# Constant products on TensorE in front of its waits, in a transformer layer with routed experts

## The chip, the cores and the metric

The kernel runs on one core of one Trainium2 chip. The metric is the time of one execution on the device, in microseconds (us), as the median of several runs. The engines are TensorE (PE; its weight loads are PEld), VectorE (DVE), ScalarE (ACT), GpSimd (POOL) and SyncE (SP), which issues most of the DMAs. TensorE's clock has two levels here, 1.2 and 2.4 GHz; the profile gives the granted level as a share of the full one (0.50 or 1.00).

## The reference

It is one transformer layer on 8 sequences of 256 tokens of width 256. Cut to what matters:

```
mod = (silu(c) @ wmod)                   # six rows a sequence: shifts, scales, gates
h = layernorm(x) * (1 + ca) + sa
q, k, v = h @ Wq.T, h @ Wk.T, h @ Wv.T   # 8 heads, 2 of keys and values, 32 wide
q, k = rope(q), rope(k); q, k, v = each normalised over its 32
p = softmax(30 * tanh((q k / sqrt(32) + mask) / 30))   # causal, window of 64
x = x + ga * ((p v) @ Wo)
h = layernorm(x) * (1 + cb) + sb
choose 4 of 16 experts for each token (best 2 of 4 groups first)
x = x + gb * (sum over the chosen of weight * expert(h) + shared expert(h))
```

## The kernel before

**Two stages.** The first function, `attention`, runs attention, the second layer norm and the choice of experts. After it all engines meet, and `experts` runs the experts. 2048 tokens are 16 tiles of 128.

**Attention** is a software pipeline over the sequences b, written out by hand: `step(b)` for b from -2 to 8. On each engine's queue one step mixes work of four sequences: `ahead` (b+2: transpose and modulate the normalised input, project it to q, k, v), `lead` (b+1: rotate, normalise, transpose q and k), `here` (b: scores, tanh, exp, times v) and `lag` (b-1: transpose the attention output, multiply by Wo, residual, layer norm, transpose, router logits). An engine's queue is strictly in order, and semaphores join the queues, so the order below is what sets the time.

PE's step is, in order: `turn_xhat(b+2)` (L807); scores of the first head group (L852 mask, L855, L858); four transposes of the attention output (L906); scores of the second group; twelve products with Wo (L791 to L793 through `split3`, which writes a float32 product as three); `weigh` of the first group (probabilities times v, L878 to L883); `project(b+2)` (L791 to L793); `weigh` of the second group; `turn_qk(b+1)`, which waits for the normalised keys (`k_done`) and transposes k (L828) and q (L838); then for `lag` a wait for the second layer norm's output (`h2_done`) and for ACT's copy of q (`qt_done`), four transposes (L941), a wait for ACT's copy of them (`h2t_done`), a wait for DVE's last attention output (`attn_done`), in steps 3, 5, 6, 7 and 8 a count of chosen rows (`count_before`, L1051 and L1052), and the router logits (L952).

DVE's step runs rotation and centring (L619 to L630), the low part of the attention output (`otl`, L726, which needs ACT's `oth`, which needs PE's L906), the residual (L669, which needs PE's Wo product), layer norms, the normalised q and k, and, in the steps named in `CHOSEN`, the 25 or so small instructions of `choose`; a step later `place_rows` (L1059 on), which needs PE's count through ACT's copy. POOL computes the powers for the norms (L431 and others), half of the rotation (L427), splits weights in the first steps, and sends rows to their experts' places in device memory (L1073).

Before PE can multiply a tile by routed weights, the last two tiles of rows must be counted (`count_before` at u = -2 of `experts`), DVE works out tables of tiles, and PE spreads them over the partitions (L1481, at u = 0). The units u are pairs of a tile and an expert: 16 units of shared tiles first, then 80 routed tiles, then 16 units of shared tiles.

**The tiles that the change touches.** `sc_ps` holds the scores: four PSUM banks of 512 float32 columns, of which columns 0 to 319 (`SC` = 320) are used. `up` holds two banks for an expert's first product, of which columns 0 to 351 are used. `ident` is the 128 x 128 identity, `mask_f` the float32 mask. Both are float32, and a plain float32 product is made of two instructions in the trace (x2 for one product).

Of the kernel before, what the change touches and what calls it, by code (L numbers as in the profile page):

```python
# [18 lines left out]
P = 128  # L19
B, S, HID = 8, 256, 256  # L20
# [4 lines left out]
REP = H // KV  # L25
# [10 lines left out]
E, INTER, TOPK, G, TOPK_G = 16, 176, 4, 4, 2  # L36
# [44 lines left out]
K1, K0, SC = 128, 192, 320  # L81
# [43 lines left out]
GROUPS = [(0, 4), (4, 4), (8, 2), (10, 2), (12, 2), (14, 2)]  # L125
LAST = len(GROUPS) - 1

CHOSEN = {3: 0, 5: 1, 6: 2, 7: 3, 8: 4}
SENT = {4: (0, 1), 5: (2, 3), 6: (4, 5), 7: (6, 7, 8), 8: (9, 10, 11)}

# [8 lines left out]
for _m in range(len(GROUPS) + 1):  # L139
    for _step in (ROUTE1 + " " + ROUTE2 if _m <= LAST else TABLES).split():  # L140
        _name, _, _times = _step.partition("*")
# [112 lines left out]
def attention(nc, a, mod_rows, x1d, rows_d, hrow, gate_t, ident, w, r):  # L254
    with ExitStack() as ctx:
# [521 lines left out]
        def _(pe):  # L777
# [6 lines left out]

            counted = pv[:, QT * E:3 * QT * E].rearrange("p (t e) -> p t e", e=E)

            def split3(out_ap, xh, xl, wh, wl):

                n = len(xh)
                for k in range(n):  # L790
                    pe.matmul(out_ap, xh[k], wh[k], start=(k == 0), stop=False)  # L791
                    pe.matmul(out_ap, xh[k], wl[k], start=False, stop=False)
                    mm = pe.matmul(out_ap, xl[k], wh[k], start=False, stop=(k == n - 1))  # L793
                return mm
# [13 lines left out]
                mm.then_inc(s.xhat_t, 1)  # L808

            def project(b):  # L810
                pe.wait_ge(s.htl_done, b + 1)
                pe.wait_ge(s.hth_done, (b + 1) * KC)
                if b == 0:
                    pe.wait_ge(s.wqkvl_done, 1)
                after(pe, s.qkv_done, b)
                after(pe, s.kt_done, b - 1)
                after(pe, s.gated_done, b - 2)
                for t in range(QT):
                    mm = split3(qkv_ps[:, t, 0:QKV], [hth[:, c, t * P:(t + 1) * P] for c in range(KC)], [htl[:, c, t * P:(t + 1) * P] for c in range(KC)],
                                [wqkvh[:, c] for c in range(KC)], [wqkvl[:, c] for c in range(KC)])  # L820
                mm.then_inc(s.qkv_mm, 1)

            def turn_qk(b):
                pe.wait_ge(s.k_done, (b + 1) * QT * KV)
                pe.wait_ge(s.qkv_done, min(b + 2, B))
                for t in range(QT):
                    for c in range(KV):
                        mm = pe.transpose(qkv_ps[:, 0, c * S + t * P:c * S + (t + 1) * P], kn[:, t, c].rearrange("p r d -> p (r d)"), ident[:])  # L828
                mm.then_inc(s.k_t, 1)
                pe.wait_ge(s.q_done, b + 1)  # L830
                if b + 1 < B:
                    pe.wait_ge(s.ht_done, (b + 2) * KC)
                    pe.wait_ge(s.hth_done, (b + 2) * KC)
                after(pe, s.oth_done, b - 1)
                after(pe, s.otl_done, b - 1)
                for t in range(QT):
                    for c in range(KV):
                        mm = pe.transpose(tp[:, c, t * P:(t + 1) * P], qn[:, t, c * P:(c + 1) * P], ident[:])  # L838
                mm.then_inc(s.q_t, 1)
# [46 lines left out]
            def step(b, ahead, lead, here, lag):  # L886
                if ahead:
                    turn_xhat(b + 2)
                if b == B:
                    pe.wait_ge(s.gate_done, b - 1)  # L890
                    pe.wait_ge(s.attn_done, 2 * b)
                    pe.wait_ge(r.placed, LAST - 1)
                    count_before(pe, r, g, counted, LAST - 1).then_inc(r.counted, 1)
                if here:
                    scores(b, b % 2, 0)
# [35 lines left out]
                if lead:  # L931
                    turn_qk(b + 1)
                if lag:
                    pe.wait_ge(s.h2_done, b)
                    if lead:
                        pe.wait_ge(s.qt_done, b + 2)
# [5 lines left out]
                    mm.then_inc(s.h2_t, 1)  # L942
                    pe.wait_ge(s.h2t_done, b)
                    if here:
                        pe.wait_ge(s.attn_done, 2 * b + 2)
                    else:
                        pe.wait_ge(r.placed, LAST)
# [128 lines left out]
def experts(nc, a, out, mod_rows, x1d, rows_d, y_d, hrow, gate_t, tab, w, r, ident):  # L1076


    with ExitStack() as ctx:
# [316 lines left out]
        def _(pe):  # L1396
            held = {}

            def load_expert(u):
                kind, i = jobs[units[u][0]]  # L1400
                if kind == "routed":
                    held[u] = nc.values_load(tab.expert[0:1, i:i + 1], engines=[mybir.EngineType.PE], min_val=0, max_val=E - 1,
                                             skip_runtime_bounds_check_because="held to E - 1 when worked out")
# [65 lines left out]
            def step(u):  # L1469
                if starts(u + 2):  # L1470
                    turn_x(units[u + 2][0])
                if 0 <= u < N:
                    up_mm(u)
                if u == -2:
                    count_before(pe, r, g, counted, LAST)
                    pe.wait_ge(r.worked, WORKED["cum", QT, LAST])
                    pe.matmul(totals, r.ones[:], r.cum[:, NT], start=True, stop=True).then_inc(r.counted, 1)
                if u == 0:
                    pe.wait_ge(r.worked, WORKED["cols", 2, LAST + 1])
                    for j in range(2):  # L1480
                        mm = pe.matmul(spread_ps[:, j], cols[0:TILES, j:j + 1].to_broadcast([TILES, P]), ident[0:TILES, 0:TILES], start=True, stop=True)  # L1481
                    mm.then_inc(s.spread, 1)
# [50 lines left out]
```

## Time and profile before

| | |
|---|---|
| median of 3 runs | 552.26 us (552.13 to 553.73) |
| the profiled execution | 552.77 us, its span 550.9 us |
| mean granted clock | 0.83 |
| PE, PEld busy | 416.4 us (76%), 379.5 us (69%) |
| DVE busy | 388.4 us (71%) |
| POOL, ACT busy | 286.8 us (52%), 234.2 us (43%) |

The span is from the first to the last instruction of the profiled execution. Its time lies 1.9 us above its span. The attention stage ends at about 274 us, the steady part of the experts runs from about 306 to 500 us, and the rest collects and stores. A busy engine in the profile isn't always one that sets the time: the question at every point is which wait ends last.

### The profile page before, as it was taken

The numbers are of one execution on the slowest core, as the hardware profiler recorded it, in microseconds if no ns is written. First come the engines' busy times: TensorE is split into PE (matmuls) and PEld (weight loads), VectorE is DVE, ScalarE is ACT, GpSimd is POOL, SyncE is SP. The second block draws the span as 40 slices with busy tenths as digits, with TensorE's granted clock in tenths as the row PEclk, the third lists the DMA queues.
The fourth block names the chain that finished last, engine by engine and source line by source line (L and its number), as shares of the span: only waits on it lengthen the run. The fifth ranks groups of instructions, "written<-read, shape, count | busy, mean of one in ns | idle before, by whom it ended". The sixth has DMA issues, their size and how long they took to land.

```text
span 550.9 us, 10571 instructions
## 1 busy us (share of the span) xinstructions
PE 416.4 (76%) x2841; PEld 379.5 (69%) x2841; DVE 388.4 (71%) x1158; ACT 234.2 (43%) x554; POOL 286.8 (52%) x278
## 2 busy tenths in 40 slices
PE   2447896966598586774234999999999999996752
PEld 2335875846486465563234998999999999986752
DVE  1663798778897968185482788777777777754998
ACT  1334362443257150400122676666666666653220
POOL 1545655633588748363376332444444444444992
PEclk9975686879598766565657899999999999999797
DMA  8404012030215122721283333444444444446962
GB/s 308 131 2 149 0 47 94 1 95 1 93 45 180 43 92 78 271 94 54 70 304 130 91 114 94 142 137 144 138 141 142 143 143 139 152 121 230 397 236 73
DMA packets 38294, 69.68 MB, mean 126 GB/s; under 512 B 5720, under 2 KB 27864, under 8 KB 38112
## 3 DMA queue, kind: packets, MB, share of 16 engines
q1 hardware_dynamic: 31328, 49.08, 28.0%
q0 software_dynamic: 6912, 19.93, 9.7%
q8 instruction: 27, 0.44, 0.3%
q14 instruction: 27, 0.22, 0.1%
HBM read 42.49 MB, written 26.51 MB: 125 GB/s over the span
## 4 chain that ended last, share of the span: by engine, by line
issue 18%; POOL 13%; DVE 8%; PE 6%; DMA 3%; another core or an unknown queue 2%; ACT 0%; POOLq 0%; DVEq 0%; SPq 0%; ACTq 0%
POOL y_d L1211 13%; DMA y_d<-yout,to 2%; DVE yt L1319 2%; DMA yt<-y_d 1%; PE up L1439 1%; DVE f_htl L1303 1%; PE up L1440 1%; PE up L1441 1%; DVE hid L1299 1%; PE xt_ps L1422 1%; DVE yt L1316 1%; DVE yt L1312 1%; PE y_ps L1463 0%; DVE f_xl L1274 0%
## 5 line engine op out<-in xcount | busy, mean ns | idle before, releaser
L1211 POOL DMA_INDIRECT y_d<-yout,to x80 | 76.7, 959 | 90.8 <-ACT yout L1246 90.0
L1073 POOL DMA_INDIRECT rows_d<-hrow,slots x64 | 65.6, 1026 | 35.5 <-issue 16.5
L1296 DVE SCALAR_TENSOR_TENSOR hid<-silu,xin,up 128x64 f32<-128x64 f32 (+1 forms) x160 | 47.2, 336 | 23.0 <-PE ht_ps L1449 16.3
L1225 ACT ACTIVATE f_xh<-xt_ps 128x256 fp32r<-128x256 f32 x96 | 36.9, 384 | 57.0 <-PE xt_ps L1422 43.6
L1230 ACT ACTIVATE silu<-up 128x176 f32<-128x176 f32 x112 | 35.6, 318 | 58.5 <-PE up L1441 44.9
L1439 PE MATMUL up<-w_routed,f_xh 128*128 x160 | 58.3, 364 | 0.0
L431 POOL TENSOR_TENSOR rn<-meansq,minus_half 128x24 f32<-128x24 f32 x8 | 33.4, 4175 | 39.5 <-DVE meansq L637 39.4
L1441 PE MATMUL up<-w_routed,f_xh 128*128 x160 | 51.7, 323 | 0.0
L1440 PE MATMUL up<-w_routed,f_xl 128*128 x160 | 51.6, 323 | 0.0
L1274 DVE TENSOR_TENSOR f_xl<-xt_ps,f_xh 128x256 fp32r<-128x256 f32 x96 | 40.6, 423 | 10.4 <-ACT f_xh L1225 4.2
L1303 DVE TENSOR_TENSOR f_htl<-ht_ps,f_hth 128x256 fp32r<-128x256 f32 x112 | 46.6, 417 | 0.0
L1235 ACT ACTIVATE f_hth<-ht_ps 128x256 fp32r<-128x256 f32 x112 | 43.1, 385 | 4.0 <-PE ht_ps L1449 3.7
L1463 PE MATMUL y_ps<-w_shared,f_hth 112*128 112x256 f32 x32 | 12.5, 391 | 26.6 <-DVE f_htl L1303 26.5
L1246 ACT ACTIVATE yout<-y_ps 128x256 f32<-128x256 f32 x80 | 30.5, 381 | 4.0 <-DMA y_d<-yout,to 3.0
L1449 PE MATMUL ht_ps<-ident,hid 128*128 128x128 f32 x112 | 30.8, 275 | 0.0
L1448 PE MATMUL ht_ps<-ident,hid 128*128 128x128 f32 x112 | 30.7, 274 | 0.0
L1422 PE MATMUL xt_ps<-ident,xin 128*128 128x128 f32 x160 | 30.5, 272 | 0.0
L1440 PEld LDWEIGHTS up<-w_routed,f_xl 128*128 128x128 f32 x160 | 30.4, 190 | 0.0
L1439 PEld LDWEIGHTS up<-w_routed,f_xh 128*128 128x128 f32 x160 | 30.2, 189 | 0.0
L1463 PE MATMUL y_ps<-w_routed,f_hth 112*128 x80 | 29.2, 365 | 1.2 <-DVE f_htl L1303 1.0
L1441 PEld LDWEIGHTS up<-w_routed,f_xh 128*128 128x128 f32 x160 | 30.0, 188 | 0.0
L233 POOL TENSOR_TENSOR w_routed<-raw,w_routed 128x960 fp32r<-128x960 f32 x9 | 20.2, 2243 | 16.7 <-ACT w_routed L1252 16.3
(259 smaller groups left out, 1335.3 us busy)
## 6 DMA issues: line engine op xcount, KB each, us to landing
xin<-rows_d SPq DMA_DIRECT2D x80, 144.0 KB
yt<-y_d SPq DMA_DIRECT2D x16, 512.0 KB, 10.3
raw<-in_w_raw SPq DMA_DIRECT2D x13, 608.0 KB
mod<-mod_rows SPq DMA_DIRECT2D x8, 384.0 KB, 3.5
w_stage<-in_w_raw SPq DMA_DIRECT2D x5, 608.0 KB, 4.1
rows_d<-zeros SPq DMA_DIRECT2D x16, 144.0 KB
x<-in_x SPq DMA_DIRECT2D x4, 512.0 KB, 8.2
x1d<-x SPq DMA_DIRECT2D x8, 256.0 KB
```

What stands on the lines that cost most here:

```text
L1073: pool.indirect_dma_start(rows_d, bass.IndirectOffsetOnAxis(ap=r.slots[:, t, k:k + 1], axis=0), hrow[:, t], None).then_inc(r.sent[t // QT] ...
L1211: pool.indirect_dma_start(y_d, bass.IndirectOffsetOnAxis(ap=to[:, i:i + 1], axis=0), yout[:, i % YR], None)\
L1225: act.activation(xh[:, j % XB], xt_ps[:], ACT.Copy).then_inc(s.xh, 1)
L1235: act.activation(hth[:, u % 2].rearrange("p c q -> p (c q)"), ht_ps[:, u % 2, 0:2 * P], ACT.Copy).then_inc(s.hth, 1)
L1274: dve.tensor_tensor(xl[:, j % XB], xt_ps[:], xh[:, j % XB].bitcast(F32), ALU.subtract).then_inc(s.xl, 1)
L1296: dve.scalar_tensor_tensor(out=hid[:, u % HB3, to_cols], in0=silu[:, u % 2, cols], scalar=weight, in1=y, op0=ALU.mult, op1=ALU.mult).then_ ...
L1303: dve.tensor_tensor(htl[:, u % 2].rearrange("p c q -> p (c q)"), ht_ps[:, u % 2, 0:2 * P], hth[:, u % 2].rearrange("p c q -> p (c q)").bit ...
L1422: mm = pe.transpose(xt_ps[:, c], src[:, c * P:(c + 1) * P], ident[:])
L1439: pe.matmul(o, xh[:, j % XB, c], wh, start=(c == 0), stop=False)
L1440: pe.matmul(o, xl[:, j % XB, c], wh, start=False, stop=False)
L1441: mm = pe.matmul(o, xh[:, j % XB, c], wl, start=False, stop=(c == KC - 1))
L1463: pe.matmul(o, hth[0:HA, q, 0], at(HA, O2A, O2B), start=begin, stop=False)
```

## The change

A helper `fill(n)` issues n matrix products whose operands are constants and whose output columns nothing reads. In attention one is the identity times 192 columns of the float32 mask, into columns 320 to 511 of the last bank of `sc_ps`; in `experts` it is the identity times itself, 128 columns, into columns 352 to 479 of the second bank of `up`. They carry no semaphore and no wait of their own. They stand on PE's queue in front of waits that PE already had:

- before `project(1)`: 8
- in `turn_qk`, before the wait for the keys: 6 in step -1, 12 in steps 3 and 5, 6 in step 6
- before the wait for `h2_done`: 6 in steps 1 to 7, 12 in step 8
- after the wait for `h2t_done`, before the wait for `attn_done`: 3 in steps 1 to 7
- in step 8, before the count of group 4 and after its other waits: 12
- in `experts`: 16 before the count of the last group (u = -2), 8 before the wait for the tables' columns (u = 0)

```diff
+WAITS_K = {-1: 6, 3: 12, 5: 12, 6: 6}
...
+            def fill(n):
+                for _ in range(n):
+                    pe.matmul(sc_ps[:, REP - 1, SC:512], ident[:], mask_f[:, 0:512 - SC], start=True, stop=True, skip_group_check=True)
...
             def project(b):
+                if b == 1:
+                    fill(8)
                 pe.wait_ge(s.htl_done, b + 1)
...
             def turn_qk(b):
+                fill(WAITS_K.get(b - 1, 0))
                 pe.wait_ge(s.k_done, (b + 1) * QT * KV)
...
                     pe.wait_ge(r.placed, LAST - 1)
+                    fill(12)
                     count_before(pe, r, g, counted, LAST - 1).then_inc(r.counted, 1)
...
                 if lag:
+                    fill(6 if b < B else 12)
                     pe.wait_ge(s.h2_done, b)
...
                     pe.wait_ge(s.h2t_done, b)
                     if here:
+                        fill(3)
                         pe.wait_ge(s.attn_done, 2 * b + 2)
...
+            def fill(n):
+                for _ in range(n):
+                    pe.matmul(up[:, 1, 2 * INTER:2 * INTER + P], ident[:], ident[:], start=True, stop=True, skip_group_check=True)
...
                 if u == -2:
+                    fill(16)
                     count_before(pe, r, g, counted, LAST)
...
                 if u == 0:
+                    fill(8)
                     pe.wait_ge(r.worked, WORKED["cols", 2, LAST + 1])
```

## Rows read from the trace of the kernel before

**Rows 1.** The page, the granted clock in 40 equal slices, in tenths
```profile
PEclk9975686879598766565657899999999999999797
```

**Rows 2.** Busy time by stretch: PE, PEld, DVE, ACT, POOL, granted clock, DMA
```profile
87.40:101.00 13.60, 11.00 (x65) 7.80 (x66) 9.11 (x15) 7.25 (x11) 2.27 (x5) 0.50 0.28 95
101.10:114.60 13.50, 10.40 (x85) 9.93 (x83) 11.91 (x28) 3.59 (x6) 12.78 (x11) 1.00 0.01 2
...
210.40:234.10 23.70, 16.86 (x94) 13.18 (x94) 9.75 (x41) 7.32 (x10) 11.91 (x12) 0.50 0.58 203
```

**Rows 3.** Whom PE waited for, 60 to 300: total, times, longest
```profile
PE tp L941 <- DVE hrow L698: 17.2, 5, 5.9
PE qkv_ps L828 <- DVE kn L651: 15.9, 3, 6.8
```

**Rows 4.** PE in order of time, steps 1 and 2: start, us, what [idle before]
```profile
88.28 1.12 PE L941 MATMUL tp<-ident,hrow 128*128 128x128 f32 x4 [2.76 <-DVE hrow L698]
90.80 1.86 PE L952 MATMUL pv<-wgate,late 128*128 128x16 f32 x8 [1.40 <-DVE attn L663]
92.50 1.09 PE L807 MATMUL tp<-ident,xhat 128*128 128x128 f32 x4
93.38 1.27 PE L852 MATMUL sc_ps<-mask,ident_b 128*128 128x320 bf16 x4
...
97.40 1.25 PE L852 MATMUL sc_ps<-mask,ident_b 128*128 128x320 bf16 x4 [0.31 <-ACT capped L519]
...
99.95 0.58 PE L791 MATMUL qkv_ps<-woh,oth 128*128 128x256 f32 x1
```

**Rows 5.** PE in order of time, step 4 and the start of 5
```profile
153.84 0.72 PE L852 MATMUL sc_ps<-mask,ident_b 128*128 128x320 bf16 x4 [0.78 <-issue]
...
155.25 0.39 PE L791 MATMUL qkv_ps<-woh,oth 128*128 128x256 f32 x1
...
166.54 0.63 PE L941 MATMUL tp<-ident,hrow 128*128 128x128 f32 x4 [0.89 <-ACT qt L507]
167.86 1.07 PE L952 MATMUL pv<-wgate,late 128*128 128x16 f32 x8 [0.69 <-ACT late L565]
168.77 0.63 PE L807 MATMUL tp<-ident,xhat 128*128 128x128 f32 x4
169.24 1.18 PE L852 MATMUL sc_ps<-mask,ident_b 128*128 128x320 bf16 x4
```

**Rows 6.** ACT in order of time, step 2
```profile
96.11 1.24 ACT L519 ACTIVATE capped<-sc_ps 128x1280 f32<-128x1280 f32 x1 [0.55 <-PE sc_ps L858]
```

**Rows 7.** DVE in order of time: the waits that PE's work ends
```profile
97.86 0.69 DVE L726 TENSOR_TENSOR otl<-tp,oth 128x512 fp32r<-128x512 f32 x1 [3.58 <-ACT oth L546]
...
102.16 0.69 DVE L669 TENSOR_TENSOR late<-qkv_ps,mod 128x512 f32<-128x512 f32 x1 [1.24 <-PE qkv_ps L793]
...
123.10 0.69 DVE L726 TENSOR_TENSOR otl<-tp,oth 128x512 fp32r<-128x512 f32 x1 [3.57 <-ACT oth L546]
...
197.76 0.22 DVE L1059 TENSOR_TENSOR place<-placed,small 128x64 f32<-128x64 f32 x1 [4.25 <-ACT placed L513]
...
234.45 0.69 DVE L669 TENSOR_TENSOR late<-qkv_ps,mod 128x512 f32<-128x512 f32 x1 [4.28 <-PE qkv_ps L793]
...
261.19 0.69 DVE L669 TENSOR_TENSOR late<-qkv_ps,mod 128x512 f32<-128x512 f32 x1 [3.02 <-PE qkv_ps L793]
```

**Rows 8.** PE in order of time, step 1: float32 products of 132 columns
```profile
76.63 0.39 PE L878 MATMUL pv<-v,masked 128*128 128x132 f32 x2
76.86 0.97 PE L880 MATMUL pv<-v,probs 128*128 128x33 f32 x8
```

**Rows 9.** PE in order of time, ahead of the routed tiles
```profile
280.16 0.19 PE L1051 MATMUL route_ps<-cum,ones 128*128 128x32 bf16 x1 [5.49 <-DVE cum L1028]
...
287.28 1.14 PE L1481 MATMUL route_ps<-ident,l_cols 80*128 80x80 f32 x4 [2.70 <-DVE l_own_e L1350]
```

**Rows 10.** ACT in order of time, the second stage's start
```profile
300.24 0.32 ACT L1230 ACTIVATE silu<-up 128x176 f32<-128x176 f32 x1 [8.02 <-remote]
```

## The prediction, made before the changed kernel was run

> **What bounds the kernel now.** I read the granted clock over the span first. It is full in the experts' steady part, but in attention and up to about 306 us it falls again and again to half [rows 1]. The table by stretch shows what surrounds a fall: at half clock from 87.4 to 101.0 PE was busy 11.00 of 13.6 us, at full clock from 101.1 to 114.6 10.40 of 13.5 [rows 2]. So a slow stretch is not one in which PE had little to do: it is one that follows a gap. The list of waits names the gaps: 17.2 us in 5 waits for DVE's `hrow` ahead of L941, 15.9 us in 3 waits for `kn` ahead of L828 [rows 3]. PE sits idle there, the clock falls, and the products behind the gap run at 1.2 GHz. The logits that end step 1 start at 90.80 and step 2's L807 at 92.50, 1.70 us later; at the end of step 4, at 2.4 GHz, the same takes 167.86 to 168.77, 0.91 us [rows 4, 5].
>
> Slow PE work costs only where another engine waits for it. DVE's own order of time shows where: in step 2 it waits 3.58 us ahead of `otl`, which hangs on PE's L906 through ACT, and 1.24 us ahead of the residual, which hangs on the Wo product; in step 3, 3.57 us; in step 6, 4.25 us for the placed rows; in step 7, 4.28 us and in step 8, 3.02 us for the Wo product [rows 7]. Between these waits DVE is the bound, and PE's clock is of no account. A mean clock of 0.83 over 550.9 us is 94 us of clock lost, but it can't come back as 94 us of time: I count the waits alone.
>
> **What a fill costs.** The nearest row is L878, a float32 product of 132 columns, which takes 76.63 to 76.86, 0.23 us, at 2.4 GHz [rows 8]. In proportion to columns, 192 are 0.33 us and 128 are 0.22 us; at 1.2 GHz twice that, 0.67 and 0.45. So at full clock 3 fills are 1.0, 6 are 2.0, 8 are 2.7, 12 are 4.0 us; the experts' 16 are 3.6 and 8 are 1.8 us. Bounds: if weight loads rather than columns paced them, all would cost the 0.23 of the row, down to 1.4 us for 6; and double at half clock.
>
> What lies over them: L941 of step 1 waits 2.76 us and the logits 1.40 more [rows 4], so 2.0 and 1.0 are hidden. L941 of step 4 waited only 0.89 us [rows 5]: there 6 fills stand out by 1.1 us and 3 more by 1.0, since the three come behind ACT's copy and the logits had waited for nothing else. The 12 in front of the keys lie in waits of up to 6.8 us [rows 3]. The 16 of the experts lie in 5.49 us and the 8 in 2.70 us [rows 9]; at half clock they would be 7.1 and 3.6, that is 1.6 and 0.9 too long. The 8 ahead of `project(1)` and the 6 of step -1 stand before POOL's and DVE's long start-up, off the path either way: 0.
>
> **What a full clock gives**, if the fills hold it:
> - Step 2, up to `otl`: the logits and L807 take 2.58 us at half clock (90.80 to 93.38) and 1.38 at full (167.86 to 169.24) [rows 4, 5]: 1.2. ACT's tanh then no longer waits 0.55 for the scores [rows 6]. Together 1.75. The wait of 1.24 ahead of the residual goes too, since the second scores fall from 2.55 (97.40 to 99.95) to 1.41 (153.84 to 155.25). Sum 3.0.
> - Step 3: the same first part, 1.75.
> - The waits for placed rows at the start of steps 4, 6, 7 and 8 (4.25 in step 6 [rows 7]): the logits and L941 ahead of them give back 0.8 and 0.45 each, the 3 fills take 1.0, and where 6 fills stand out by 1.1 the faster transposes of q and k return about that. I count 1.5 for the four; the bounds are 5.0 (no fill in the way) and -3 (each stands out in full while the clock is slow).
> - Step 7: first scores 1.15, second scores 1.15, the Wo product 1.2 of the 4.28 [rows 7]: 3.5.
> - Step 8: of the 3.02 behind `otl` the twelve products are nearly all, 1.2 of it comes back; L906 0.3. Sum 1.5. The last L941 and logits count nothing: the wait ahead of them is 5.9 us [rows 3], 12 fills fill 4.0, and the clock may well have fallen again.
> - Start of the experts: L1481 0.57 of its 1.14 [rows 9], and as an estimate 0.9 from the first dozen products behind it, whose kind halves as L852 does. Sum 1.5.
>
> All of it is 12.75 us. Steps 2 and 3 I take whole, 4.75, because PE's clock was full ahead of their gaps [rows 2, 8] and need only be held. The rest, 8.0, I take at half: there the clock has to be won back first, gaps of 2 to 3 us stay even with the fills, and each slow fill costs double. That is 4.0, in all 8.75. From the profiled execution's 552.77 this gives 544.0; the median of the runs lies 0.5 lower, so 543.5 us. The experts' steady part isn't touched, since it runs at full clock with PE full, and everything behind shifts by what the start gains.
>
> The Trainium skill, TensorE: Matmul & The Clock Gate, Part 1 (The HAM clock gate), has a rule that speaks against this: it puts the ramp penalty below 1% of a typical kernel's span. By that rule this change could give no more than 5.5 us, 546.8 or above; rows 1 show falls all through attention, not one ramp, so the trace agrees with it only for the experts' steady part.
>
> **Rivals.**
> - *A small gain or none.* The fills don't hold the clock: PE does only short transposes ahead of and behind them, and a 6.8 us wait with 4.0 us of fills still has 2.8 idle. For it: the clock fell behind 114.6 although PE had been busy for 10.40 of the 13.5 us before [rows 2]. Against: fills are as dense as work gets. Steps 2 and 3 then give half, 2.4, and of the rest what the standing out of fills takes: 549.5, and 547.5 to 552 around it. This is also the case in which the change doesn't do what it says. The skill's rule above is of this kind; its own bound is 546.8.
> - *A stall goes as well.* ACT's silu at 300.24 comes after 8.02 idle us that the trace can't put down to an engine [rows 10], though the unit's products take only some 2 us. If it hangs on the order of events, a new timing may lose it: 8 us more and about 1.5 that PE's clock loses in it, 534. Against: nothing in the change aims at it.
> - *Slower.* The fills are issued while the clock is at 1.2 GHz and stay so: 6 take 4.0 us against 0.89 of wait in step 4 [rows 5] and, as I take it, in 5 and 6 (3.1 each, 9.4), and 3 take 2.0 in about five steps (10): 552.3 + 19 = 571. It decides where a fill run lasts longer than its wait, above 2.8 us for steps 1 and 2. Against: in each gap of steps 1 and 2 the clock is still full when the fills begin.
>
> **How the numbers follow.** Forecast (539 to 547.5) 0.55; stall gone too 0.17; small gain or none 0.20, half of it within 0.3% (1.7 us, about what a measurement can tell from no change); slower 0.08. So faster 0.82, same 0.10, slower 0.08. The range runs from 532 (all of the 12.75 and most of the stall) to 551.
>
> **What would show it.** In the changed kernel's profile the clock row should read 9 or more over most of attention; L952 to L807 should be about 0.9 us apart in every step; DVE's waits of rows 7 should shrink to about 1.8, 0, 1.8, 4, 1 and 1.8 us; L941 should start later behind L838 in steps 4 to 6, by about 1 us. The prediction is wrong if the clock still falls in steps 4 to 8, if the gain in DVE's waits is eaten by new waits for POOL's powers (L431) or for `placed`, or if the 8 us stall moves.

## The result, and the profile after

The changed kernel took 561.16 us (560.11 to 564.62, 4 runs) against 552.96 us for the kernel before (552.13 to 553.73, 4 runs). The ratio is 1.0157, interval 1.0129 to 1.0185: 8.2 us slower, where 9 us less was forecast. The profiled execution has a span of 559.2 us, against 550.9. Here and below the ratios leave out executions more than 1.5% above the fastest of their kernel and the medians do not, so a ratio need not be the quotient of the medians beside it.

The granted clock did what it was meant to do up to about 190 us, and in part behind that. The page of the changed kernel, its clock row and the group of the fills (262 float32 instruction records, 377 ns mean):

```profile
PEclk9989689999999886667877799999999999999787
...
L792 PE MATMUL sc_ps<-mask_f,ident 128*128 128x192 f32 x262 | 57.0, 377 | 6.3 <-ACT late L567 5.8
```

Where [rows 1] have 5 to 9, slices 6 to 15 (of 14.0 us each) read 9 and 8 now, while 16 to 23 still read 6 to 8. The stretches (columns as in [rows 2]) say the same in numbers: at full clock from 87.4 to 187 us, 0.72 behind that.

```profile
87.40:101.00 13.60, 10.88 (x102) 8.79 (x100) 11.11 (x18) 8.63 (x12) 4.26 (x6) 1.00 0.26 94
...
140.00:187.00 47.00, 38.97 (x331) 35.21 (x332) 38.23 (x115) 20.30 (x29) 35.06 (x35) 1.00 0.31 105
187.00:234.00 47.00, 36.94 (x220) 33.13 (x220) 22.24 (x75) 10.28 (x16) 21.72 (x20) 0.72 0.38 129
```

DVE's own waits, which answer to [rows 7], show both halves of the story: the two waits ahead of `otl` fell from 3.58 and 3.57 to 1.58 us, and the waits for the placed rows (`place`, which stands behind L941, now L953, and the logits) grew, one of them to 14.27 us. Line numbers of the changed kernel are higher by up to some 20.

```profile
96.65 0.69 DVE L728 TENSOR_TENSOR otl<-tp,oth 128x512 fp32r<-128x512 f32 x1 [1.58 <-ACT oth L548]
118.44 0.69 DVE L728 TENSOR_TENSOR otl<-tp,oth 128x512 fp32r<-128x512 f32 x1 [1.58 <-ACT oth L548]
195.31 0.23 DVE L1072 TENSOR_TENSOR place<-placed,small 128x64 f32<-128x64 f32 x1 [5.79 <-ACT placed L515]
...
232.12 0.19 DVE L1072 TENSOR_TENSOR place<-placed,small 128x32 f32<-128x32 f32 x1 [14.27 <-ACT placed L515]
...
257.69 0.19 DVE L1072 TENSOR_TENSOR place<-placed,small 128x32 f32<-128x32 f32 x1 [6.74 <-ACT placed L515]
```

What holds the second of these `place` is seen in PE's and ACT's order of time. First PE of the changed kernel (L792 are the fills, L838 and L848 the transposes of the keys and queries):

```profile
213.33 4.19 PE L792 MATMUL sc_ps<-mask_f,ident 128*128 128x192 f32 x12
217.31 1.06 PE L838 MATMUL qkv_ps<-ident,kn 128*128 128x128 f32 x4
218.16 0.71 PE L848 MATMUL tp<-ident,qn 128*128 128x128 f32 x4
218.71 2.12 PE L792 MATMUL sc_ps<-mask_f,ident 128*128 128x192 f32 x12
225.94 1.08 PE L953 MATMUL tp<-ident,hrow 128*128 128x128 f32 x4 [5.12 <-ACT qt L509]
227.71 2.29 PE L792 MATMUL sc_ps<-mask_f,ident 128*128 128x192 f32 x6 [0.69 <-ACT late L567]
```

then ACT, whose copies of the transposed keys and queries L953 waits for:

```profile
223.81 0.60 ACT L507 ACTIVATE kt<-qkv_ps 128x512 f32<-128x512 f32 x1 [20.21 <-remote]
225.20 0.60 ACT L509 ACTIVATE qt<-tp 128x512 f32<-128x512 f32 x1 [0.79 <-remote]
```

The keys' transposes end at 218.37 and ACT had been idle for 20 us, but it starts its copy at 223.81. Its releaser reads `remote`: the trace finds no engine's increment there in time. The semaphore events of the trace tell more. The increment that L838's last instruction makes is recorded at 223.73, 5.4 us after that instruction's end, and L848's at 225.18, 6.3 us after 218.87. The increments of ACT, DVE and POOL that can be matched stand 0.01 us behind the ends of their instructions (median; none is over 0.04), and so do nearly all of PE's. I call such increments of PE late. The ends of PE's products in the profile are modelled, so the trace doesn't tell a product that truly finished late from an increment that was passed on late; but PE itself had gone on to the next instructions (L848 at 218.16, the fills at 218.71).

The same thing in the experts' first units: the products of the second unit end at 295.80, their increment comes 11.6 us later, and ACT's silu answers to the stall of [rows 10] with twice its length.

```profile
291.15 0.32 ACT L1243 ACTIVATE silu<-up 128x176 f32<-128x176 f32 x1
307.43 0.32 ACT L1243 ACTIVATE silu<-up 128x176 f32<-128x176 f32 x1 [15.96 <-remote]
```

The kernel before has them too: products that end between 292.4 and 293.8 have increments 6.6 to 7.8 us late, all at 300.2 to 300.4. That is the stall of [rows 10]; in attention it has three, 1.1 to 2.1 us late, of products that end between 223 and 227.

### The profile page after: what moved, and what is told of

It is laid out like the page before. It is cut to its first block and busy times, and to the rows that moved or that the text cites. A ratio compares the mean times of both kernels' runs of the same rounds, so it can differ in the third digit from the quotient of the medians.

```text
span 559.2 us, 11187 instructions
## 1 busy us (share of the span) xinstructions
PE 448.9 (80%) x3151; PEld 418.6 (75%) x3151; DVE 388.4 (69%) x1158; ACT 233.6 (42%) x554; POOL 285.8 (51%) x278
## 5 line engine op out<-in xcount | busy, mean ns | idle before, releaser
L1224 POOL DMA_INDIRECT y_d<-yout,to x80 | 76.7, 959 | 90.9 <-ACT yout L1259 89.8
L1309 DVE SCALAR_TENSOR_TENSOR hid<-silu,xin,up 128x64 f32<-128x64 f32 (+1 forms) x160 | 47.2, 336 | 23.2 <-PE ht_ps L1467 19.7
L792 PE MATMUL sc_ps<-mask_f,ident 128*128 128x192 f32 x262 | 57.0, 377 | 6.3 <-ACT late L567 5.8
L792 PEld LDWEIGHTS sc_ps<-mask_f,ident 128*128 128x128 f32 x262 | 51.7, 225 | 8.2 <-ACT late L567 7.7
L1457 PE MATMUL up<-w_shared,f_xh 128*128 128x352 f32 x64 | 23.6, 369 | 12.4 <-DVE hid L1312 12.4
L1457 PEld LDWEIGHTS up<-w_routed,f_xh 128*128 128x128 f32 x160 | 30.2, 189 | 0.0
```

Of the source, the lines that this page charges most:

```text
L792: pe.matmul(sc_ps[:, REP - 1, SC:512], ident[:], mask_f[:, 0:512 - SC], start=True, stop=True, skip_group_check=True)
L1224: pool.indirect_dma_start(y_d, bass.IndirectOffsetOnAxis(ap=to[:, i:i + 1], axis=0), yout[:, i % YR], None)\
L1309: dve.scalar_tensor_tensor(out=hid[:, u % HB3, to_cols], in0=silu[:, u % 2, cols], scalar=weight, in1=y, op0=ALU.mult, op1=ALU.mult).then_ ...
L1457: pe.matmul(o, xh[:, j % XB, c], wh, start=(c == 0), stop=False)
```

## The experiments

Runs that were made together met the same chip, and each ratio is against the kernel before on that chip. The chips turned out not to be alike, so each run names its chip (A, B, C, D); which one the first result was made on isn't on record. A table comes first: the lengths in the trace from one L941 to the next (1 to 2 is from step 1's to step 2's, and so on), from step 8's L941 to the choice that starts the experts, from there to the first send of y, and the rest. The start-up ahead of step 1's L941 varies from 87.2 to 91.0 us from one execution to another (step6 has 90.5, step6_2, the same kernel, 87.4) and is left out. It isn't without effect on what follows: without early fills 1 to 2 takes 25.4 or 25.5 where it was 87.4 to 88.6, and 23.6 to 24.0 in the three profiles where it was 90.1 to 90.9 (before_zeros, step6_late, step6).

```
              chip  1-2   2-3   3-4   4-5   5-6   6-7   7-8  choice  y send  rest
before         -    25.4  31.2  21.6  27.1  25.8  26.7  20.9   7.0    63.4   213.5
after          -    21.8  29.5  21.8  29.3  34.5  26.0  22.0   7.0    65.9   212.4
exp_only       A    25.5  31.3  21.6  27.1  25.8  26.7  20.9   7.0    64.5   217.8
att_only       A    21.7  29.5  24.2  29.1  31.6  27.1  21.3   7.0    63.1   213.8
early5         A    21.8  29.5  24.2  27.7  26.5  25.0  20.9   7.0    63.6   212.0
wide           A    21.8  32.1  23.8  27.3  32.8  24.9  19.7   7.0    63.4   213.2
bf16           A    21.8  29.5  21.7  30.3  35.1  28.0  22.6   7.0    66.4   212.5
after_zeros    A    21.8  29.5  21.8  29.0  35.1  28.0  22.0   7.0    65.7   213.2
after_sends    A    21.8  29.5  21.8  30.4  35.2  26.0  26.8   7.0    65.3   212.3
before_zeros   A    23.6  31.5  21.7  27.9  26.7  25.8  20.9   7.0    63.2   213.2
before_2       D    25.4  31.2  21.6  27.1  25.8  26.8  20.9   7.0    63.4   212.8
early5_2       D    21.8  29.5  21.8  29.3  26.7  24.5  21.0   7.0    63.9   211.5
before_late    B    25.4  31.2  21.6  27.1  25.6  24.0  20.8   4.2    91.5   214.7
step6_late     B    24.0  33.2  21.6  27.1  26.5  20.8  20.8   4.2    90.7   212.0
step6          B    23.8  31.5  21.7  26.8  26.3  21.0  20.9   7.0    57.0   213.5
few_wide       B    21.8  31.6  21.7  28.9  25.4  22.4  20.9   7.0    60.0   211.9
step6_2        C    25.5  31.3  21.6  27.1  26.5  21.0  20.9   7.0    59.7   211.4
few_wide_2     C    21.8  29.5  23.2  28.6  25.4  22.4  21.0   7.0    60.0   211.5
after_2        C    21.8  29.5  21.8  29.3  29.1  21.1  19.0   7.0    60.5   211.8
wide_2         C    23.9  31.7  23.8  29.0  28.5  20.9  22.7   7.0    58.7   212.4
```

**One half each.** att_only keeps the fills in attention, exp_only those of the experts:

```diff
 # att_only
-                    fill(16)          # u == -2
-                    fill(8)           # u == 0
 # exp_only: all fill(...) of attention taken out
```

> The fills of attention alone; those in front of the two waits of the experts stage are gone. In the changed kernel the steps up to 5 gain (the logits of step 4 start 3.4 us sooner), step 6 then loses: the increments of TensorE that follow the transposes of k and q at 217 to 219 us arrive 5.4 and 6.3 us after the recorded ends. Theory late signals (TensorE's increments come late while GpSimd sends rows back to back, and the more instructions TensorE has issued in that time the later): step 6 loses as before and the stall at the start of the experts goes back to about 8 us, so about 559 us. Theory overhang (the fills simply outlast their waits, the late increments are a coincidence of one trace): the loss of step 6 is about 2 us, so 555 to 557 us.

> The 16 and 8 fills of the experts stage alone. Theory late signals: the stall begins one or two units sooner, since 24 float32 products are 96 more instructions while GpSimd sends 16 times in a row; its end is tied to GpSimd's last send. Loss 2 to 4 us, 555 to 557 us. Theory overhang: 16 fills outlast their wait by at most 1.6 us and part of that is hidden, the products behind run at 2.4 GHz: 552 to 553.5 us.

Measured: att_only 559.44 against 553.57, 1.0093 (1.0062 to 1.0124); exp_only 554.20 against 553.57, 1.0013 (0.9989 to 1.0036). The loss is mostly attention's, from 5 to 6 on. The experts' fills are worth nothing by the ratio and cost time in the traces: 1.1 us up to the first send of y when they stand alone (64.5 against 63.4), 2.8 on top of attention's (65.9 against 63.1). They run when the clock has mostly fallen, at 0.58 from 281.3 to 287.6. The changed kernel, ahead of the routed tiles:

```profile
281.30 6.28 PE L1415 MATMUL up<-ident 128*128 128x128 f32 x32
287.42 0.18 PE L1064 MATMUL route_ps<-cum,ones 128*128 128x32 bf16 x1
...
290.22 1.95 PE L1415 MATMUL up<-ident 128*128 128x128 f32 x16
```

**Only the early steps.** early5 leaves out what stands behind step 5, and the experts' fills.

```diff
-                fill(WAITS_K.get(b - 1, 0))
+                fill(WAITS_K.get(b - 1, 0) if b - 1 <= 5 else 0)
-                    fill(12)
-                    fill(6 if b < B else 12)
+                    fill(6 if b <= 5 else 0)
-                        fill(3)
+                        fill(3 if b <= 5 else 0)
```

> Fills of attention in steps -1 to 5 alone, none from step 6 on and none in the experts stage. Both theories: the gain of about 3 us that the changed kernel has at the end of step 4 is kept in part (its step 5 loses 1.8 us of it by six fills that stand out behind the transposes of q). Theory late signals: 550 to 551.5 us. Theory overhang: the same. If it is at 552.5 or above, a gain in front of step 6 is always absorbed later.

Measured: 552.43 against 553.57, 0.9948 (0.9905 to 0.9991). The ten executions spread from 546.01 to 558.34, and these medians are only 0.2% apart, so the whole gain isn't firm. In the lengths the gain is plain and stands in the first steps (21.8 and 29.5 against 25.4 and 31.2); with what is put in from step 6 on, the changed kernel loses more than that. One thing is seen at L952's fills of step 3, the same three in both kernels. early5:

```profile
142.34 2.29 PE L792 MATMUL sc_ps<-mask_f,ident 128*128 128x192 f32 x6 [0.69 <-ACT late L567]
144.42 0.26 PE L1063 MATMUL pv<-cum,ones 128*128 128x64 bf16 x1
```

and the changed kernel:

```profile
141.70 1.24 PE L792 MATMUL sc_ps<-mask_f,ident 128*128 128x192 f32 x6 [0.69 <-ACT late L567]
142.78 0.19 PE L1064 MATMUL pv<-cum,ones 128*128 128x64 bf16 x1
```

Three fills cost 2.08 us at half clock and 1.08 at full; where the clock happens to stand when they begin is worth 2.4 us in 3 to 4 (24.2 against 21.8).

**Fewer and more instructions for the same columns.** If the late increments depend on how many instructions PE issues, fewer and wider fills should lose less, and more of them more. wide makes them of 512 columns (3/8 of the instructions in attention, 1/4 in the experts); bf16 makes four bf16 products of each, which is twice the instructions that a float32 product leaves in the trace, over the same columns.

```diff
 # wide
-                for _ in range(n):
-                    pe.matmul(sc_ps[:, REP - 1, SC:512], ident[:], mask_f[:, 0:512 - SC], ...)
+                for _ in range((3 * n + 4) // 8):
+                    pe.matmul(sc_ps[:, REP - 1, :].rearrange("p (a n) -> p a n", n=P), ident[:], ident[:].unsqueeze(1).to_broadcast([P, 4, P]), ...)
 ... # experts: n // 4 of 512 columns
 # bf16
+                if n:
+                    pe.wait_ge(s.mask_set, 2)
+                for _ in range(4 * n):
+                    pe.matmul(sc_ps[:, REP - 1, SC:512], ident_b[:], mask[:, 0:512 - SC], ...)
 ... # experts: 4 * n of r.before[:], r.before[:]
```

> The same places and about the same TensorE time, but each fill is one product of 512 columns (the identity four times) where there were 8/3 of 192, or 4 of 128: 3/8 or 1/4 of the instructions. Theory late signals with instructions as the load: the lateness of step 6 shrinks from 6.3 to 1 or 2 us and the stall of the experts back to about 8 us: 553 to 555 us. Theory overhang: TensorE's time is the same, so 561 us.

> The changed kernel with each float32 fill replaced by four bf16 products of the same columns (constants of bf16): the same columns through the array, twice the instructions. If the number of TensorE's instructions while GpSimd sends is what delays its increments, step 6 loses 10 us or more and the stall begins sooner: 565 us or more. If only columns or time count, 561 us, as the changed kernel.

Measured: wide 555.88 against 553.57, 1.0071 (1.0038 to 1.0104); bf16 569.45 against 552.89, 1.0319 (1.0277 to 1.0360). In the order of instructions it reads wide, changed kernel, bf16: 1.007, 1.016 (1.020 on chip A with the zero writes moved, below), 1.032. Step 6's late increments of the keys and queries are 1.3 and 3.8, 5.4 and 6.3, 7.5 and 7.1 us. Two things weaken the upper end. The profiled executions of bf16 and of the changed kernel with the zero writes moved are alike (spans 564.3 and 564.0 us, 35.1 us from 5 to 6 in both), and bf16 was not run on a chip without late increments, so its other costs aren't separated. The experts' part of wide is no proof either, since its stall (7.89 us ahead of one silu) is as long as that of the kernel before.

**Is it SyncE's zero writes?** They run at that time too. Two runs move the 16 writes of `rows_d` on SyncE's queue ahead of its loads of sequence 2 and later: after_zeros in the changed kernel, before_zeros in the kernel before.

```diff
+            sp.wait_ge(s.zeros_set, 1)
+            for e in range(E):
+                sp.dma_start(rows_d[e * CAP:e * CAP + P], zeros[:]).then_inc(s.heads_zeroed, 16)
             for b in range(2, B):
...
-            sp.wait_ge(s.zeros_set, 1)
-            for e in range(E):
-                sp.dma_start(rows_d[e * CAP:e * CAP + P], zeros[:]).then_inc(s.heads_zeroed, 16)
```

> The changed kernel with SyncE's 16 writes of zeros moved from the end of its attention queue (218 to 228 us, beside GpSimd's 12 sends in a row) to before its loads of step 2. If the backlog of small transfers delays TensorE's increments and the zeros are the larger part of it, the 5.4 and 6.3 us of step 6 fall below 1 us and the time to 553 to 555 us. If GpSimd's sends alone do it, the increments stay 5 to 6 us late and the time at 560 to 562 us. The stall at the start of the experts stage, where no zeros are written, stays in both.

> The same move of the zeros in the kernel before. If the zeros delay the increments, its own late ones at 223.2, 225.6 and 226.6 us (1.5, 2.1 and 1.1 us) go: 549 to 551 us. If the sends alone do it, no change, 552 to 554 us.

Measured: after_zeros 564.29 against 552.89, 1.0202 (1.0146 to 1.0258); before_zeros 553.97, 1.0018 (0.9984 to 1.0052). The late increments stay: 3.6 to 4.5 us in step 6 of after_zeros, where silu's stall is 16.00 us, and up to 3.1 at 227 to 230 in before_zeros. The zero writes aren't needed for them.

**Is it POOL's sends?** All late increments (over 0.1 us) lie in times when POOL sends rows one behind the other: in each of the 12 profiles that have them three or more sends start in the 8 us ahead of such an increment, the last of them at most 4.0 us ahead. In step 6 of the changed kernel there are 12 sends with 0.30 us between them, from 208 to 223 us, the first and the last of them:

```profile
208.02 1.06 POOL L1086 DMA_INDIRECT rows_d<-hrow,slots  x1 [0.18 <-DVE sig L998]
...
222.21 0.96 POOL L1086 DMA_INDIRECT rows_d<-hrow,slots  x1 [0.30 <-issue]
```

and the keys' late increment comes at 223.73. after_sends moves the sends of tiles 4 and 5 from step 6 to step 7. step6_late and before_late move all sends of tiles 4 to 11 behind attention; step6 is the partner of step6_late and has the fills of step 6 alone.

```diff
 # after_sends
-SENT = {4: (0, 1), 5: (2, 3), 6: (4, 5), 7: (6, 7, 8), 8: (9, 10, 11)}
+SENT = {4: (0, 1), 5: (2, 3), 7: (4, 5, 6, 7), 8: (8, 9, 10, 11)}
 # step6_late, before_late
+SENT = {4: (0, 1), 5: (2, 3)}
-for t in range(12, NT):
+for t in range(4, NT):
 # step6: WAITS_K = {6: 6}, fill(6) and fill(3) in step 6 only, no other
```

> The changed kernel with GpSimd's eight sends of tiles 4 and 5 moved from step 6 to step 7, so that nothing is sent while TensorE runs the fills of step 6 and transposes q and k. If the sends (with or without the zeros) delay the increments, the 5.4 and 6.3 us at 218 us go, and part of it comes back in step 7, where 16 sends now stand in a row: 554 to 560 us. If the sends have nothing to do with it, 561 us with the same late increments.

> The kernel before with the fills of step 6 alone: 6 before the keys, 6 before h2_done, 3 before attn_done. Theory late signals: the whole loss of step 6 is here, the increments behind the transposes of k and q are 3 to 6 us late, the time from L941 of step 5 to L941 of step 6 grows from 25.8 to about 32 us: 558 to 561 us. Theory that the late increments need the clock or the shift that the earlier fills bring: 555 us or less.

> The same fills of step 6, but GpSimd sends tiles 4 to 11 in the experts stage with the last four, so that it sends nothing from step 6 on in attention (the experts stage then waits longer for its rows; the total says nothing alone). Theory late signals by sends: in step 6 and later no increment is over 0.3 us late, and step 6 takes at most 2 us longer than in the kernel before with sends moved in the same way. If the fills alone delay the increments, they are 3 to 6 us late as before.

> The control: the kernel before with the sends of tiles 4 to 11 moved to the experts stage. Theory late signals: its own late increments of 1.1 to 2.1 us at 223 to 227 us go and the attention stage ends about 3 us sooner, at about 271 us; at the start of the experts the stall becomes much longer, since 48 sends in a row take 60 us: 30 us or more over the kernel before in total. Otherwise the attention stage ends at 274 us as before.

Measured: after_sends 566.73 against 552.89, 1.0242 (1.0198 to 1.0286). It tells nothing of its question, since POOL still sent one behind the other from 210 to 225 us, and the keys' and queries' increments are 5.5 and 5.1 us late; it only made 7 to 8 longer (26.8). The other three met chip B and gave a surprise. The kernel before took 545.70 us there, not 553, step6 542.72, 0.9961 (0.9937 to 0.9985), step6_late 573.97 and before_late 575.68 (1.0560 and 1.0594, the price of sends that no longer hide behind attention). And in none of the three is a single matched increment of PE late by over 0.06 us, step6 with all its sends in place included. So these don't answer the question of the sends either; they raise that of the chip. In before_late, the kernel before with no late increments, the second stage starts like this:

```profile
284.88 0.32 ACT L1230 ACTIVATE silu<-up 128x176 f32<-128x176 f32 x1 [5.37 <-PE up L1441]
...
286.54 0.32 ACT L1230 ACTIVATE silu<-up 128x176 f32<-128x176 f32 x1
```

The releaser is PE's product by name, not `remote`, and the 8 us stall of [rows 10] isn't there.

**The same kernels on other chips.** few_wide puts wide fills only where the trace shows the clock full ahead of a gap (5 ahead of the keys of step 3; 2, 2 and 3 ahead of L941 of steps 1 to 3; 1 ahead of the logits of steps 1 and 2). Then four kernels were run on chip C, all as they had been.

```diff
 # few_wide, in units of the old fills: 12 are 5 wide ones, 8 are 3, 6 are 2, 3 are 1
+WAITS_K = {3: 12}
+                    fill({1: 6, 2: 6, 3: 8}.get(b, 0))
+                        fill({1: 3, 2: 3}.get(b, 0))
```

> Only fills that lie in their waits and before GpSimd's sends begin, as products of 512 columns: 5 before the keys in step 3, 2, 2 and 3 before h2_done in steps 1 to 3, 1 before attn_done in steps 1 and 2. The gain of the changed kernel up to step 4 (3.4 us at its logits) should stay to the end: 549 to 550.5 us. If it doesn't, something between step 4 and the end absorbs an earlier arrival.

> The few wide fills before the sends begin. On the second chip it was 542.5 against 545.7. On the first, 549 to 551 us against 553.

> The changed kernel again. The last four kernels ran on another chip of the pool than all the others, and there the kernel before took 545.7 us where it took 553 before, with no increment of TensorE more than 0.06 us late. Theory late signals, by chip: on such a chip the changed kernel gains, 536 to 541 us against 545.7; on the first chip it loses as before, 561 against 553. Theory overhang: it loses on both, about 2% or at least 1%.

> The fills as products of 512 columns, all places. On a chip without late increments the number of instructions is of no account: the same time as the changed kernel within 1.5 us. On the first chip again about 5 us under the changed kernel.

> The fills of step 6 alone. On the first chip theory late signals expects 557 to 560 us against 553 (step 6 is where the increments were 5 to 6 us late); on the second it was 542.7 against 545.7 and should be that again.

Measured: few_wide on B 542.51 against 545.70, 0.9941 (0.9899 to 0.9983), on C 543.94 against 545.09, 0.9962 (0.9925 to 0.9998). after_2, the changed kernel on C: 542.84 (540.30 to 546.16, 12 runs) against 545.09 (541.38 to 553.39, 35 runs), 0.9971 (0.9937 to 1.0005). wide_2 548.52, 1.0064 (1.0036 to 1.0092). step6_2 543.34, 0.9979 (0.9948 to 1.0010). The interval of the changed kernel's reaches 1.0005, so its gain isn't clear of nothing. No increment of PE is late on C either. On that chip the changed kernel is 18 us faster than in the first result, and step 6 of it reads, on PE and on ACT:

```profile
214.90 4.19 PE L792 MATMUL sc_ps<-mask_f,ident 128*128 128x192 f32 x12
218.88 0.87 PE L838 MATMUL qkv_ps<-ident,kn 128*128 128x128 f32 x4
219.59 0.60 PE L848 MATMUL tp<-ident,qn 128*128 128x128 f32 x4
220.02 2.12 PE L792 MATMUL sc_ps<-mask_f,ident 128*128 128x192 f32 x12
221.98 0.60 PE L953 MATMUL tp<-ident,hrow 128*128 128x128 f32 x4
```

```profile
219.85 0.60 ACT L507 ACTIVATE kt<-qkv_ps 128x512 f32<-128x512 f32 x1 [14.79 <-PE qkv_ps L838]
220.34 0.59 ACT L509 ACTIVATE qt<-tp 128x512 f32<-128x512 f32 x1
```

ACT starts 0.1 us behind the end of the keys' transposes, and L953 follows the fills at once, where it waited for 5.12 us before. wide_2 loses in another way: its fills left the clock to fall in steps 1 to 3 (its logits of step 1 took 1.72 us against 1.06 in few_wide_2), so its lengths up to 3 to 4, and 7 to 8, are longer. Wide fills are no general remedy. But the two kernels side by side are the best evidence on the number of instructions: wide is at 1.0071 on A and 1.0064 on C, no worse where increments are late, while the changed kernel is at 1.0157 in the first result and 0.9971 on C.

**The kernel before once more, for its profile,** and early5 beside it. No diff: both as they were.

> The kernel before itself, for its profile on whichever chip it meets. Theory (late increments of TensorE belong to a chip): if the median is near 545 us, the profile shows no matmul increment over 0.1 us late, the third silu of the experts starts at about 286 and the choice ends (DVE's start of the last choice) at about 268.5; if it is near 553, it shows increments over 1 us late at 222 to 227 us and at 292 to 294, and silu at about 300. Rival (the stall is part of the kernel, and only the median differs by chip): silu at 300 in either case.

> Attention fills in steps up to 5 alone, again. Theory (fills ahead of full clocked stretches gain, those of step 5 on give it back): against before on the same chip 1 to 3 us faster, logits of step 3 at 142.5 to 144.5 (before 147.3). On a chip without late increments the choice starts at 266 to 268 against 268.5, as few_wide had 266.1. Rival (only the first steps' fills gain and those of steps 4 and 5 cost as much): no difference, choice at 268.5.

They met a fourth chip, D. before_2 took 552.57 us (10 runs; the kernel before 554.29 as its partner, 0.9978, interval 0.9957 to 0.9998, so two samples of one kernel differ by that much), and its profile shows late increments at the places of the first profile: 4.4, 2.2 and 1.2 us at 223 to 227, 6.7 to 8.0 in the experts, and the stall.

```profile
300.64 0.32 ACT L1230 ACTIVATE silu<-up 128x176 f32<-128x176 f32 x1 [8.13 <-remote]
```

early5_2 took 550.29 (4 executions: 545.27, 546.26, 554.33 and 556.25, so without an interval), its profiled span is 544.4 against 550.5. Its profile, of the one of 546.26, has late increments (1.7 and 1.8 us, of products that end at 217.7 and 222.1, and the stall), so these don't by themselves part the two pairs of times; what does stays open.

So where the kernel before takes about 553 us (A, D and the first result) increments are late and the stall is there; where it takes about 545 (B, C) they aren't and it isn't. That holds in all the 20 profiles.

**Is it the recording?** The same split runs through what the traces hold. The 12 profiles with late increments have 5,696 to 5,856 records of semaphore updates, the 8 without have 7,848 to 7,866. The changed kernel has 5,735 in the first result and 7,848 on C, with the same 11,187 records of instructions. Up to 140 us, ahead of POOL's first send of rows at 146, the two traces are alike (876 and 873); from 140 to 500 us they hold 3,723 and 6,032. The page shows it where it can't find landings: of the changed kernel,

```profile
xin<-rows_d SPq DMA_DIRECT2D x80, 144.0 KB
rows_d<-zeros SPq DMA_DIRECT2D x16, 144.0 KB
```

and of after_2, with the time to landing in us,

```profile
xin<-rows_d SPq DMA_DIRECT2D x80, 144.0 KB, 2.1
rows_d<-zeros SPq DMA_DIRECT2D x16, 144.0 KB, 3.2
```

So on chips A and D records are lost from where the sends begin, and late increments begin there too (the changed kernel's first is at 149). A rival that nothing here rules out is therefore that the taking of the trace holds PE's increments up: more instructions and more landings are also more records. Every execution on record has a span and a granted clock, and none is there that was surely not recorded, so whether the 8 us and the 10 us exist in an unrecorded execution stays open. The loss also limits the matching: on A and D some of PE's increments have no record, and a late one among them would be missed.

## Why the prediction was wrong

**The step that failed** is a sentence of a rival. Of the stall of [rows 10] I wrote "Against: nothing in the change aims at it", and took it for a thing of 8 us that could only stay or go. It is one case of late increments, these are later in the kernels that have PE issue more, and I had put some 300 more matmul instructions on PE (3,151 against 2,841 in the trace), six fills right ahead of the transposes whose increments matter. The sum had no term for that. Against the same kernel without late increments the changed kernel pays for them:

- 5 to 6: 34.5 against 29.1, 5.4 us; 6 to 7: 26.0 against 21.1, 4.9; 7 to 8: 22.0 against 19.0, 3.0; the experts' start: 65.9 against 60.5, 5.4. Together 18.7, and the medians differ by 18.3 (561.16 and 542.84).
- The kernel before pays 2.7 (26.7 against 24.0) in 6 to 7 and 3.7 at the experts' start (63.4 against the 59.7 of step6_2, which has no fills there; step6 has 57.0), 6.4 or more in all, and the medians differ by some 8.

The difference, 18.3 less 8, is 10 us: that is the surprise. That "the 8 us stall moves" was among the prediction's signs of being wrong, but only its going had a price. Why increments are late stays open. The surprise was not foreseen by "Slower" either. That rival had the fills themselves stand out for 19 us at half clock, and what took the time is increments, which no row of fills shows.

**The rest of the error** is seen with the late increments gone. There the medians are 2.25 us apart (0.9971, interval to 1.0005), not 9. By the table, after_2 against the kernel before (before_late up to 7 to 8, as its attention is the kernel before's but for the sends):

| | forecast | measured |
|---|---|---|
| step 2 | 3.0 | 3.6 |
| step 3 | 1.75 | 1.7 |
| waits for placed rows of steps 4, 6, 7 and 8 | 1.5, at half 0.75 | -0.2 (3 to 4), -2.2 (4 to 5), -3.5 (5 to 6) |
| step 7 | 3.5, at half 1.75 | 2.9 |
| step 8 | 1.5, at half 0.75 | 1.8 |
| start of the experts | 1.5, at half 0.75 | -0.8 |
| sum | 8.75 | 3.3 |

- *Steps 2 and 3* were right in mechanism and size: DVE's waits ahead of `otl` came to 1.58 (forecast 1.8), that ahead of the residual of step 2 to nothing. Part of the 3.6 may be luck, since 1 to 2 takes 23.6 to 24.0 in three profiles without early fills.
- *The price of a fill* was right: 6 at full clock 0.33 each (2.12 us for 12 instruction records, less the overlap), at half 0.67 (213.33 to 217.31).
- *The waits for placed rows* had the wrong sign, and this is the step of the working that failed on every chip. I counted 6 fills that stand out "by 1.1" and took it back from faster transposes. But the fills ahead of `h2_done` stand behind the keys' transposes in every step, and the second layer norm's rows (`hrow`) were ready before they ended. In after_2 `hrow` of step 5 is done at 190.4, and L953 starts at 192.91, when the fills end:

```profile
189.83 3.24 PE L792 MATMUL sc_ps<-mask_f,ident 128*128 128x192 f32 x12
192.91 0.60 PE L953 MATMUL tp<-ident,hrow 128*128 128x128 f32 x4
194.20 1.24 PE L792 MATMUL sc_ps<-mask_f,ident 128*128 128x192 f32 x6 [0.69 <-ACT late L567]
```

2.5 us stand out where I had 1.1. In step 6 more does: `hrow` is done at 218.7, while the 6 ahead of the keys run at half clock (4.0 us, 214.90 to 218.88), so the keys are late, then 6 more follow, and L953 starts at 221.98, 3.3 us behind its rows. In before_late the same distance is 0.7 us in both steps, so the fills add 1.8 and 2.6. DVE's waits for `place` behind L953 of steps 5 and 6 in the same execution, where the kernel before has 4.25 [rows 7] and, without late increments (before_late), 4.20:

```profile
196.76 0.22 DVE L1072 TENSOR_TENSOR place<-placed,small 128x64 f32<-128x64 f32 x1 [5.79 <-ACT placed L515]
...
225.79 0.19 DVE L1072 TENSOR_TENSOR place<-placed,small 128x32 f32<-128x32 f32 x1 [6.55 <-ACT placed L515]
...
231.24 0.69 DVE L671 TENSOR_TENSOR late<-qkv_ps,mod 128x512 f32<-128x512 f32 x1 [1.98 <-PE qkv_ps L800]
```

What these fills buy is on the third line: the wait for the Wo product falls from 3.79 (before_late) to 1.98, and with it 6 to 7 by 2.9. In step 6 that is less than the fills cost ahead of it; step6 and step6_2, which have no fills in the first steps, pay only 0.7 and 0.9 for the same 2.9 and 3.0 and are 2.2 and 2.1 ahead over the two lengths (0.9961 and 0.9979 in all; the second one's interval reaches 1.0010).
- *Part of 4 to 5 isn't the fills'.* few_wide_2 and few_wide have none there and take 28.6 and 28.9 against 27.1, and few_wide_2 takes 23.2 against 21.6 in 3 to 4 (few_wide 21.7). What is gained in steps 2 and 3 is partly given back; by what isn't separated.
- *The experts' start*: 16 fills took 6.28 us in a wait of 5.49, mostly at half clock (7.1 was the bound given), and exp_only shows a loss of 1.1 us in that part.
- *The clock* had to be won back from step 4 on, which the forecast took at half; it was 0.82 from 187 to 281 us in after_2, and 0.72 and 0.75 in the two halves of that stretch in the first profile.

Where increments aren't late, what came back is 0.3%, and 0.6% at most in the best of the variants. The Trainium skill (TensorE: Matmul & The Clock Gate, Part 1) puts the ramp penalty below 1% of a typical kernel's span. The runs lie within that bound, which would have been the better forecast of the gain; but the sentence is on the ramp, and the clock here fell many times, so they don't test it.

## What to carry to other kernels

Filler products are not free even in a stretch where PE only waits: they delay what comes behind them when the other engine turns out to be early, they cost double when the clock has fallen already, and on some chips PE's own increments came later with them. I would put them only where the clock is still full and the wait is longer than they are at half clock; here six such places gave 0.4 to 0.6% (two runs of one kernel once differed by 0.2%), all of them together 0.3% or a loss of 1.6%. A wait whose releaser reads `remote` behind finished work is not a fixed cost: look at the semaphore events, compare the increment's time with the end of the instruction that makes it, compare how many records of semaphore updates two traces of one kernel hold, and run it on another chip before pricing it.

## What the runs showed of the hardware

- **Late increments.** On chips A and D, and in the first profiles, increments of PE's matmuls come up to 12.6 us behind the recorded end of the instruction, several at once when they come; ACT's, DVE's and POOL's don't. They occur in this kernel from POOL's first sends of rows on, an indirect transfer each 1.26 us: in attention from step 4 on, at the start of the experts, and, by 1.2 us at most, at 487 to 510 us, when POOL sends rows of y. At the experts' start the engine that waited goes on 3.4 to 4.0 us behind the start of POOL's last send of rows in all 12 such profiles, bf16 included, whatever PE did in between. That POOL's sends cause it is only argued: the kernels that took them away ran on chip B, where nothing is late with the sends in place either.
- **Lost records.** The same 12 profiles lack about a quarter of the records of semaphore updates (5,696 to 5,856 against 7,848 to 7,866), all of it behind 140 us. Whether the recording holds the increments up, or both have one cause, stays open.
- **Chips differ.** One and the same kernel takes 552.6 to 554.3 us on two chips and 545.1 to 545.7 on two others, and a change to it is 1.0157 (first result) or 0.9971 (C). What differs between the chips stays open.
- **Two executions of one kernel** differ by up to 3 us before step 1 ends (87.4 and 90.5 us at L941 in step6_2 on C and step6 on B; 88.6 in before_late, the same code up to there, on B too), so a gain of 2 us needs many runs, or the lengths of single stretches.
